# Edge stage of layer 0 in rounds of 32 edge tiles instead of 16, with another order of work on every engine

## The reference, cut to what matters

```python
q = (feat @ Wq.T + bq).reshape(n, H, D)
k = (feat @ Wk.T + bk).reshape(n, H, D)
v = (feat @ Wv.T + bv).reshape(n, H, D)
e = jnp.einsum('ehd,ehd->eh', q[src], k[dst]) * scale
m = jax.ops.segment_max(e, dst, num_segments=n)
ex = jnp.exp(e - m[dst])
denom = jax.ops.segment_sum(ex, dst, num_segments=n)
sa = ex / denom[dst]
agg = jax.ops.segment_sum(sa[:, :, None] * v[src], dst, num_segments=n)
```

## Time and profile before

| what | value |
|---|---|
| median of 3 runs | 7137.76 us (7133.32 to 7147.25) |
| the profiled execution's own time | 7156.78 us |
| its span, first to last instruction | 7154.9 us |
| mean granted clock of PE | 0.792 |
| the edge stage of layer 0 in it | about 1053 to 2546 us |
| first spans of a round, last spans, end of the last add | 1130.4, 2519.4, 2542.8 us |

### The profile page before, as it was taken

One profiled execution on the slowest core, in us unless ns is written; L12 is line 12 of the kernel. 1 busy time (PEld: TensorE's weight loads), 2 busy tenths in 40 slices (PEclk: granted clock), 3 DMA queues, 4 the chain that ended last, 5 costly groups with the idle time before them and its releaser, 6 DMA issues. The chain is left out here.

```text
span 7154.9 us, 86877 instructions
## 1 busy us (share of the span) xinstructions
PE 4895.2 (68%) x21453; PEld 3505.2 (49%) x21454; DVE 3944.3 (55%) x9373; ACT 2616.2 (37%) x5007; POOL 3190.5 (45%) x3260
## 2 busy tenths in 40 slices
PE   4468366777777778378877753354555556999999
PEld 3246134555555578345555453333344334666565
DVE  4257136899888966312221287466666666444443
ACT  0134004555555533033333331355555553222222
POOL 2641605677777657356666400466666661000000
PEclk6568797899989965588888856677777777999999
DMA  2001257788888877233333207555555553000000
GB/s 50 1 0 39 52 166 223 235 244 247 245 241 244 242 178 173 81 89 74 80 82 77 76 3 235 184 145 144 148 146 145 147 145 101 16 15 15 15 15 11
DMA packets 616359, 852.88 MB, mean 119 GB/s; under 512 B 209716, under 2 KB 419611, under 8 KB 615645
## 3 DMA queue, kind: packets, MB, share of 16 engines
q0 software_dynamic: 159136, 383.90, 20.7%
q1 hardware_dynamic: 319069, 416.84, 18.5%
q10 hardware_dynamic: 137972, 50.36, 3.0%
HBM read 692.81 MB, written 164.74 MB: 120 GB/s over the span
## 5 line engine op out<-in xcount | busy, mean ns | idle before, releaser
L1340 POOL DMA_INDIRECT b_got<-tmp_l_table,b_src x928 | 998.7, 1076 | 445.6 <-issue 263.8
L2444 POOL DMA_INDIRECT w_got<-tmp_l_table,w_src x928 | 878.9, 947 | 539.4 <-issue 247.7
L3158 POOL DMA_INDIRECT t_got<-tmp_f_table,t_src x672 | 634.0, 943 | 429.7 <-DVE t_sums L3236 224.2
L2693 PE MATMUL w_pa<-w_got,w_hot 128*128 128x264 f32 x1856 | 639.7, 503 | 204.1 <-issue 106.5
L1586 PE MATMUL b_pk<-b_keys,b_hot_t 128*128 x1856 | 549.4, 447 | 290.7 <-issue 179.8
L2693 PEld LDWEIGHTS w_pa<-w_got,w_hot 128*128 128x128 f32 x1856 | 436.9, 248 | 321.3 <-issue 226.6
L1586 PEld LDWEIGHTS b_pk<-b_keys,b_hot_t 128*128 128x128 f32 x1856 | 386.5, 219 | 379.3 <-issue 320.6
L3617 DVE SCALAR_TENSOR_TENSOR l_accs<-l_po,l_prob,l_accs 128x256 f32 (+1 forms) x392 | 173.5, 480 | 598.4 <-PE l_po L3723 598.4
L1601 PE MATMUL b_pa<-b_got,b_hot 128*128 128x260 f32 x1856 | 485.8, 408 | 6.7 <-issue 2.5
L3668 ACT ACTIVATE l_h<-l_ph,l_bn 128x896 f32<-128x896 f32 x224 | 245.0, 1096 | 661.9 <-PE l_ph L3713 661.9
L3272 PE MATMUL t_ph<-t_xt,t_w 128*128 128x448 f32 x896 | 406.5, 599 | 110.5 <-issue 110.4
(11 more groups left out here) (570 smaller groups left out, 9993.9 us busy)
## 6 DMA issues: line engine op xcount, KB each, us to landing
tmp_g_acc<-b_acc SPq DMA_DIRECT2D x232, 260.0 KB
w_spread<-tmp_g_rel_rows SPq DMA_DIRECT2D x232, 256.0 KB
t_spread<-tmp_f_rel_rows SPq DMA_DIRECT2D x170, 256.0 KB
b_spread<-tmp_g_rel_rows SPq DMA_DIRECT2D x116, 256.0 KB
e_attr<-in_edge_attr ACTq DMA_DIRECT2D x103, 256.0 KB
tmp_f_experts<-t_y SPq DMA_DIRECT2D x28, 896.0 KB
yl_y<-tmp_f_experts SPq DMA_DIRECT2D x28, 896.0 KB, 10.9
b_got<-tmp_l_table,b_src POOLq DMA_INDIRECT x928
```

Of the source, the lines that this page charges most:

```text
L1340: pool.indirect_dma_start(out=got[:, m % NB, u, :], out_offset=None, in_=T["l0_table"], in_offset=bass.IndirectOffsetOnAxis(ap=src[:, m * ...
L2444: pool.indirect_dma_start(out=got[:, p % 3, u, :], out_offset=None, in_=T["l1_table"], in_offset=bass.IndirectOffsetOnAxis(ap=src[:, p * R ...
L2693: mm = pe.matmul(pa[:, (k * RS + n) % SUMS, 0:WV], hot[:, (k * B4 + b) % 3, u - b * U, :], got[:, k, u, 0:WV], start=(u == 2 * n), stop=(u ...
L3158: pool.indirect_dma_start(out=got[:, g % DEPTH, u, :], out_offset=None, in_=T["f_table"], in_offset=bass.IndirectOffsetOnAxis(ap=src[:, g ...
```

## The change

Inside `stage_l0_edges` alone R becomes 32: 29 rounds of 8 batches and 16 stops, the 32 tiles times 4 heads on all 128 lanes. The instructions for each batch keep their shapes and their number. The instructions for each round halve in number; `picked` (L1475) is 128x64 instead of 128x32, the chain is 65 long instead of 33, the ends are 128x32 instead of 128x16. The ring keeps twelve slots. The one-hot matrices `hot` keep four buffers (HOTS), `hot_t` three. The tile numbers of a round are 16 values at an offset of 16p instead of 8 at 8p + 2, and PE uses them for `expand(0)` at once. Batches 0 to 5 of round p are now weighed and summed in round p itself, batches 6 and 7 in round p + 1 (LATER = 6); before, all of them were weighed in round p + 1. In PE's order `expand(0)` of the next round now comes ahead of `chain_ends`. The spreads come in quarters of a round. Three memsets in the set-up go. The diff, cut to its core:

```diff
+    R = 32
+    ROUNDS, RS = L.steps // R, R // 2
...
+    HOTS = 4
     LOOP = 3
-    TIMES = 18
+    TIMES = 9
+    LATER = 6
...
-        spread = s.sb("spread", [P, 2, B4 // 2, U * P], BF16)
+        spread = s.sb("spread", [P, 2, 2, U * P], BF16)
-        hot = s.sb("hot", [P, B4, U, P])
+        hot = s.sb("hot", [P, HOTS, U, P])
...
ACT
+                if behind:
+                    make_hot(p - 1, B4 - 1)
+                if now_:
+                    make_apart(p, 0)
+                hot_t_of(1)
+                hot_t_of(2)
                 if now_:
                     act.wait_ge(drop_ready, p + 1)
                     act.activation(fade[:, :], drop[:, :], ACT.Exp, scale=SCALE).then_inc(fade_ready, 1)
+                hot_of(0)
                 if now_:
                     act.wait_ge(diff_ready, p + 1)
                     act.activation(exps[:, :], now[:, :], ACT.Exp, scale=SCALE).then_inc(exp_ready, 1)
                     act.wait_ge(weights_out, p + 1)
+                    act.activation(weight[:, :], p_fade_weight, ACT.Copy).then_inc(weights_ready, 1)
+                if ahead and now_:
                     load_masks(act, p + 1)
+                hot_of(1)
+                hot_t_of(3)
+                hot_of(2)
+                hot_t_of(4)
...
DVE
+                weigh_later(LATER)
                 if now_:
                     spans(p)
+                adds_later(10, 11)
+                weigh_later(LATER + 1)
                 if now_:
                     chains(p)
+                adds_later(12, 13)
                 if now_:
                     differences(p)
+                score_of(0)
+                adds_later(14, 15)
+                if now_:
+                    dve.wait_ge(weights_ready, p + 1)
+                weigh_of(0)
+                if now_:
+                    fade_last(p)
+                weigh_of(1)
+                score_of(1)
+                adds(0, 1)
+                score_of(2)
+                weigh_of(2)
+                adds(2, 3)
+                score_of(3)
+                weigh_of(3)
                 adds(4, 5)
+                score_of(4)
+                weigh_of(4)
+                adds(6, 7)
+                score_of(5)
+                weigh_of(5)
+                adds(8, 9)
+                score_of(6)
+                score_of(7)
...
PE
                 if now_:
                     turn_scores(p, at)
                 if ahead:
-                    tile = tiles(p + 1, 2, 10 if two_ahead else 8)
-                expand_of(1)
-                sums_of(0, 0, 1)
+                    tile = tiles(p + 1, 0, RS)
+                expand_of(0)
                 if now_:
                     chain_ends(p)
-                expand_of(2)
-                sums_of(1, 2, 3)
+                sums_later(LATER)
                 if now_:
                     spread_tops(p)
-                expand_of(3)
-                sums_of(2, 4, 5)
-                sums_of(3, 6)
+                sums_later(LATER + 1)
                 if now_:
                     turn_weights(p)
+                expand_of(1)
+                expand_of(2)
+                sums_of(0)
+                sums_of(1)
+                expand_of(3)
+                sums_of(2)
                 expand_of(4)
-                sums_of(3, 7)
+                sums_of(3)
+                expand_of(5)
+                sums_of(4)
+                expand_of(6)
+                expand_of(7)
+                sums_of(5)
```

More of the change, by code:

```diff
@@ L1514, in add, with round_, weigh_later, adds_later @@
                                          ).then_inc(added, 1)
-            def round_(p, at, turn, ahead, now_, behind, two_behind):
-                def weigh_of(b):
+            def round_(p, at, turn, ahead, now_, behind):
+                def weigh_later(b):
                     if behind:
                         weigh(p - 1, b, slot(at - 1, b))
+                def adds_later(*stops):
+                    if behind:
+                        for n in stops:
+                            add(p - 1, at - 1, n)
+                def weigh_of(b):
+                    if now_:
+                        weigh(p, b, slot(at, b))
+                def adds(*stops):
+                    if now_:
+                        for n in stops:
+                            add(p, at, n)
                 def score_of(b):
@@ L1624, in turn_weights, with round_, sums_later, sums_of @@
                 pe.transpose(p_weight, exps[:, :], K["ident"][:, :]).then_inc(weights_out, 1)
-            def round_(p, at, two_ahead, ahead, now_, behind):
-                def sums_of(b, *stops):
+            def round_(p, at, ahead, now_, behind):
+                def sums_later(b):
                     if behind:
-                        sums(p - 1, at - 1, b, slot(at - 1, b), *stops)
-                def expand_of(n):
-                    if ahead if n < B4 else two_ahead:
-                        expand(p + 1 + n // B4, at + 1 + n // B4, n % B4, tile[2 * n - 2:2 * n])
+                        sums(p - 1, at - 1, b, slot(at - 1, b), 2 * b, 2 * b + 1)
+                def sums_of(b):
+                    if now_:
+                        sums(p, at, b, slot(at, b), 2 * b, 2 * b + 1)
+                def expand_of(b):
+                    if ahead:
+                        expand(p + 1, at + 1, b, tile[2 * b:2 * b + 2])
                 if now_:
```

175 lines of the change are left out of this document (72 added, 103 removed).

## The result

The changed kernel takes 7164.22 us (median of 7 runs, 7149.03 to 7178.61) against 7135.43 us (median of 7, 7121.4 to 7147.25) for the kernel before: the ratio is 1.0041 with a 95% interval of 1.0027 to 1.0055. It is slower by 29 us where 27 us faster was forecast. The rest of the program varies by as much as this: the profiled execution of the changed kernel is one of the short ones (7149.0 us, 7147.0 of span), so the stage has to be read by itself.

What follows compares the result with a forecast made beforehand. Stage bound by DVE, POOL 8% behind; of 6.6 us won per round, two new waits return all but 0.5. Rounds -39.5 us, ends +12.4: -27 off the 7137.8 median, so 7111; range 7030 to 7190.

Steps and rivals of the forecast that it cites:

- DVE's own work: DVE's instructions per round of 32 tiles: 42.15 us against 48.74 now, winning 6.6 us a round if DVE alone decided.
- The masks, spreads and stores move the same bytes per tile ... Nothing: Transfers of a round: same bytes in half or as many issues, costed at nothing.
- step 6: Landing of the last gather before score 7: 4.0 us taken, giving DVE a second stall of 2.9 us.
- My upper bound, two gathers in front: Upper bound on the last gather's landing, with two more gathers in front of it: 5.3 us.
- Step 2, the late release: Expand 0 on PE releases its waiters about 5.85 us after its start, so DVE stalls 2.8 us before the chains.
- Steps 3 to 5: Weigh 0 starts at 14.3 us, sums 0 free the slot at 17.7, POOL's last of 16 gathers starts at 40.3.
- the 0.35 that I had added: Added to the round's 47.85 us because the same sum for today's kernel falls 0.1 to 0.3 short: 48.2.
- The load of the tile numbers: PE's load of 16 numbers ahead of expand 0: 1.2 us taken, bounds 0.6 and 3.9.
- The rival that put 3.9 on it: Slower rival: PE's load of tile numbers is paid by value, rounds of 50.9 us, total 7186; chance 0.20.
- The ends: Before the first spans 8 us more, behind the last spans 4.4 more: +12.4 us.
- that through batch 0: Loop from weigh 0 through sums 0, the freed slot, 16 gathers and landing to score 7: round of 48.2 us.
- The gathers land later: No-change rival: gathers land after 5.0 us, the round is 49.2 and the total 7139; chance 0.10.

Runs made afterwards that it cites:

- e11: The changed kernel with a round's last store, and the spread behind it, sent only when score 7 is done: 7062.21 us, ratio 0.9974 to the kernel before.
- e9: The changed kernel with weigh 6, adds 10 and 11 and sums 6 ahead of score 7; a store and spread move too: 6233.88 us, ratio 0.9948.
- e10: The changed kernel with every spread sent a second time, into a buffer nobody reads: 6243.22 us, ratio 0.9966 to the kernel before.
- e2: The changed kernel with weigh 0 ahead of score 0 on DVE and sums 0 ahead of expand 2 on PE: 6301.64 us, ratio 1.0053.
- e7: The changed kernel with chain_ends, sums 6, 7 ahead of expand 0, sums 0 before expand 1, weigh 0 before score 0, adds 0, 1 behind weigh 1: 6269.63 us.

## Why the prediction was wrong, point by point

**DVE's own work: right.** The spans and the differences took 1.59 and 1.55 us where 1.60 and 1.53 were forecast. Score, weigh, adds, and the 3.55 us behind the start of score 7 are as costed. The prediction gives ACT and PE about 30 of 48 us; for PE say 256.78 / 340 x 48.74 = 36.8. Nothing hung on it.

**"The masks, spreads and stores move the same bytes per tile ... Nothing": this is the step that failed**, and with it the 4.0 us of step 6. The bytes are the same, but the new order puts the last store and a spread (516 KB) right on the last gathers that DVE waits for. The landing was 5.7 us, and 3.8 with the store sent later (e11); e9 and the two sorts of rounds in e10 show the same on the other kind of chip. With that alone changed the round is 48.12, and 48.2 was forecast; the ratio is then 0.9974 where the forecast's 27 us would be 0.9962. That the rounds agree so closely is in part luck, because two other terms were off by 1.2 and -1.0 us there and cancel. My upper bound, two gathers in front, was 5.3, and was exceeded.

**Step 2, the late release: right that it costs, wrong where.** I put 5.85 us on expand 0 and so 2.8 before the chains; the wait there was 0.72. It fell on sums 0 instead. These end at 16.0 in the trace, 1.7 us sooner than forecast, but POOL goes on only at 19.0, 1.3 us later than forecast. On the chips without the late release POOL finds the slot free.

**Steps 3 to 5: near.** Weigh 0 started at 12.5 instead of 14.3; the sixteen gathers took 21.75 us, 22.6 were forecast. In sum: +1.3 at the slot, -0.85 for the gathers, +1.7 for the landing, and of the 0.35 that I had added some 0.15 were not there: +2.0 a round, 56 us. The ends, below, take 6 us of that back, and the 50 us that are left are the way from the forecast's -27 to the stage's +23.4.

**The load of the tile numbers: right.** 1.11 us against 1.2 taken. The rival that put 3.9 on it is excluded by the row, and so is the price per register of 200 ns from the Trainium skill (Runtime: NRT & Kernel Launch, Instruction fetch mechanics), which would give 3.2; the measurement decides. The page does not say that its price holds for a kernel's own loads from SBUF, as this one is. That the total came out close to that rival's is chance.

**The ends:** 4.7 us behind the last spans as forecast (4.4), but 1.5 and not 8 ahead of the first: the first of the six scores that wait for rows there starts at 1116.37, where its counterpart started at 1120.67, and they run nearly head to tail from then on.

**What the prediction did not have** is the loop through the slot of batch 6. With its own numbers it comes to nearly the same round as that through batch 0, so it didn't change the forecast; but on the second kind of chip it is the one that binds. Moving weigh 0 alone (e2) gained nothing that can be measured, and moving sums 6 and 7 and chain_ends ahead of expand 0 as well (e7) gained 34 us. The 70 us of e9 come mostly from what stands behind the last gather, where its edit had also moved a spread, and not from this loop.

**The rivals.** "The gathers land later" had 0.10 and is the one that came true in its mechanism, at 5.7 us instead of the 5.0 that I gave it.

## What to carry to other kernels

When a ring is shorter than two rounds of work, write down for each slot who frees it, and follow every one of these loops, not the first that comes to mind: where two are nearly as long, cutting one leaves the other. Same bytes is not same cost: look where a reordered store or copy falls against the one transfer that an engine waits for. Moving one store and the copy behind it by a few microseconds took this change from 0.4% slower to 0.3% faster (on two chips of the same kind). And look at what an edit moves besides what it is meant to move, before its gain is put down to the one thing.

## What the runs showed of the hardware that was not expected

- Two chips ran the same program in 7077 to 7135 us and four in 6268 to 6275. Much of it lies ahead of this stage: the first spans of the kernel before start at 1130.4 us on the one and at 786.5 on the other.
- On the first kind, engines that wait for PE's matmuls go on 2 to 4 us after the ends that the trace models, several at once: ACT, DVE and POOL at 1720.12, 1720.28 and 1720.47, where the expand of 1714.26 took 3.67 us. On the second kind ACT has its release 3.81 us after the same cold expand starts. No run tells the cause.
- A loop body twice as long costs this kernel about 7 us in each turn (24 us rounds become 30.5 to 32.6), with an engine at "issue" for 5.39 and 3.42 us.
- A gather lands in 3.8 us with no other transfer near it (e11) and in 5.7 to 6.4 us with a store of 260 KB and a spread of 256 KB issued within about a microsecond of it. With the store alone it is 4.0 us or less (e9).
- Sending every spread twice made the kernel 0.86% faster than the changed kernel. That its last store then falls behind the last gathers in most rounds is what the trace shows; why it shifts that way wasn't tried.
